# A tree-lookup layer on one Trainium2 core: five half-unit places for gathered rows, another order of the gathers, bias pieces kept elsewhere

## The reference, cut to what matters

```python
logits = x @ W_in.T + b_in                       # x: layer-normed tokens; HID = 4 trees x 1365 nodes x 4
act = gelu(logits); act4 = act.reshape(B, P, G, FAN)
decisions = argmax(act4, axis=-1)
for d in range(DEPTH):                            # DEPTH = 5 moves: 6 nodes for each token and tree
    moves = take_along_axis(decisions, current)
    current = next_platform + FAN * (current - platform) + moves
mask = sum(one_hot(n, G) for n in nodes)
new_logits = (act4 * mask[..., None]).reshape(B, HID) @ W_out.T
```

## Time and profile before

| | us |
|---|---|
| median of 3 runs | 2145.59 |
| lowest and highest | 2142.69, 2166.28 |
| the profiled execution | 2149.68 |
| its span in the profile | 2147.9 |
| from the first matmul of the trees layer to its last addition | 586.93 to 969.44 |

### The profile page before, as it was taken

The page is one execution under the profiler, slowest core; times in us unless marked ns, Lnnn a source line. Parts: engine busy times, 40 slices in busy tenths (PEclk is TensorE's granted clock), DMA queues, the critical chain, the costliest instruction groups (busy, mean ns, idle before and its releaser), DMA issues. The chain is left out here.

```text
span 2147.9 us, 34926 instructions
## 1 busy us (share of the span) xinstructions
PE 1648.2 (77%) x12368; PEld 1139.4 (53%) x12368; DVE 1221.2 (57%) x4315; ACT 850.6 (40%) x1792; POOL 464.6 (22%) x611
## 2 busy tenths in 40 slices
PE   3368646798878867745589979996886777999888
PEld 1147433454537656644345447763554654677666
DVE  5965645564277768642376623335766876766332
ACT  1142335355327556552245543332553420333423
POOL 0001000220022433420243100003201214655211
PEclk8655777799879988977699989986997866999979
DMA  2000001220034564640322000002211000000000
GB/s 80 0 11 1 9 29 46 71 57 19 7 112 164 207 227 158 225 169 6 102 75 76 22 16 0 0 27 64 54 33 58 1 1 1 2 2 2 2 1 21
DMA packets 79748, 115.69 MB, mean 54 GB/s; under 512 B 8416, under 2 KB 60512, under 8 KB 78816
## 3 DMA queue, kind: packets, MB, share of 16 engines
q0 software_dynamic: 18432, 67.38, 9.0%
q1 hardware_dynamic: 58560, 45.00, 7.5%
q10 hardware_dynamic: 2592, 1.18, 0.2%
HBM read 88.95 MB, written 1.05 MB: 42 GB/s over the span
## 5 line engine op out<-in xcount | busy, mean ns | idle before, releaser
L2321 POOL DMA_INDIRECT f_rows<-tree_table,f_index x128 | 132.7, 1037 | 324.8 <-DVE f_index L2377 153.4
L2534 PE MATMUL f_ps_o<-f_rows,shared_sb 128*128 128x128 f32 x1024 | 136.1, 299 | 71.0 <-ACT f_rows L2606 71.0
L2534 PEld LDWEIGHTS f_ps_o<-f_rows,shared_sb 128*128 128x128 f32 x1024 | 131.7, 212 | 76.7 <-ACT f_rows L2606 73.8
L1469 ACT ACTIVATE x_probs<-x_ps_z 128x768 f32<-128x768 f32 (+1 forms) x128 | 117.5, 918 | 104.6 <-PE x_ps_z L1334 66.4
L2606 ACT ACTIVATE f_rows<-f_rows,f_low_act 128x128 f32<-128x128 f32 x512 | 152.9, 387 | 0.8
L2416 DVE CUSTOM_DVE_ANT_0 f_rows<-f_rows,f_xn 128x128 f32<-128x128 f32 x512 | 111.4, 287 | 59.9 <-DMA f_rows<-tree_table,f_index 59.9
L1173 DVE TENSOR_REDUCE x_minus_max<-x_ps_s 128x4 f32<-128x1024 f32 x64 | 78.2, 1224 | 63.0 <-PE x_ps_s L1334 62.7
L3052 ACT ACTIVATE r_probs<-r_ps_z 128x768 f32<-128x768 f32 x64 | 51.9, 811 | 67.5 <-PE r_ps_z L2943 67.5
L1794 PE MATMUL f_ps_h<-f_xnT,weights 128*128 128x512 f32 x144 | 76.8, 661 | 2.3 <-ACT f_hT L1859 2.3
L1806 PEld LDWEIGHTS f_ps_y<-weights,f_hT 128*128 128x128 f32 x576 | 70.3, 193 | 14.3 <-issue 12.6
L1859 ACT ACTIVATE f_hT<-f_ps_h,weights 128x512 f32<-128x512 f32 x72 | 48.6, 685 | 69.8 <-PE f_ps_h L1794 68.1
(11 more groups left out here) (651 smaller groups left out, 4196.2 us busy)
## 6 DMA issues: line engine op xcount, KB each, us to landing
x_queries<-x_pieces SPq DMA_DIRECT2D x96, 64.0 KB, 2.1
x_keys<-x_pieces SPq DMA_DIRECT2D x84, 64.0 KB, 2.1
a_queries<-a_pieces SPq DMA_DIRECT2D x48, 64.0 KB, 2.1
weights<-w_L_ffn SPq DMA_DIRECT2D x1, 2985.5 KB, 10.1
a_keys<-a_pieces SPq DMA_DIRECT2D x42, 64.0 KB, 2.1
weights<-w_L_ffn SPq DMA_DIRECT2D x1, 2449.0 KB, 11.0
weights<-w_L_ffn SPq DMA_DIRECT2D x1, 2176.0 KB, 8.5
f_rows<-tree_table,f_index POOLq DMA_INDIRECT x128, 6.0
```

Source lines behind the costliest of these rows:

```text
L1469: a.activation(probs[:, r % HELD, :, :], ps_z[:, :, 0:WIDE], ACT.Exp, scale=scale).then_inc(exped, 1)
L2321: pool.indirect_dma_start(rows[:, u % 2, j, tree, :], None, g.tree_table, bass.IndirectOffsetOnAxis(index[:, u % 2, low, j * TREES + tree: ...
L2534: last = pe.matmul(ps_o[:, low, j, :], g.ident, rows[:, u % 2, j, tree, OUT + f * D:OUT + (f + 1) * D], start=k == 0, stop=k == TREES * FA ...
```

## The change

`rows` becomes a ring of five places, one half unit each, and the half (u, j) takes place (2u + j) mod 5, with a semaphore for each place. A gather for low = 0 into a place waits for the low = 1 sum of the half that held it five halves earlier. POOL's order becomes: gather(0,0,0), gather(0,0,1); then for each h gather(0,h+1,0), gather(1,h,0), gather(0,h+1,1), gather(1,h,1). `low_act` has three buffers instead of two. The bias pieces lose their own tiles: `bias_left` and `bias_part` lie in the fifth place of `rows`, `bias_rows` lies over the bias weights themselves, and so the bias is first copied to `bias_left`.

```diff
@@ -2258,6 +2258,7 @@
     LOW = DEPTH + 1 - DENSE
     OUT = FAN * D
     KEPT = 5
+    PLACES = 5
     STEPS = range(UNITS + 1)
     with ExitStack() as ctx:
         sb = lambda n, s, d=F32: ctx.enter_context(nc.sbuf_tensor("f1_" + n, s, d))
@@ -2266,14 +2267,16 @@
         xn, xnT = sb("xn", [P, KEPT, HALVES, D]), sb("xnT", [P, T])
         act = [sb("act%d" % d, [P, 2, Q, FAN ** d, FAN]) for d in range(DENSE)]
         here = [sb("here%d" % d, [P, Q, FAN ** d]) for d in range(1, DENSE)]
-        low_act = sb("low_act", [P, 2, Q, FAN])
+        low_act = sb("low_act", [P, 3, Q, FAN])
         value, rank_of = sb("value", [P, Q, FAN]), sb("rank_of", [P, Q, FAN])
         peak, node = sb("peak", [P, Q]), sb("node", [P, 2, Q])
         index = sb("index", [P, 2, LOW, Q], U32)
         maskedT = sb("maskedT", [P, ALL, P])
-        bias_rows, ones_rows = sb("bias_rows", [3, sum(WIDTHS)], BF16), sb("ones_rows", [3, P], BF16)
-        bias_left, bias_part, kept = sb("bias_left", [3, sum(WIDTHS)]), sb("bias_part", [3, sum(WIDTHS)]), sb("kept", [3, 3])
-        rows = sb("rows", [P, 2, HALVES, TREES, ROW])
+        ones_rows, kept = sb("ones_rows", [3, P], BF16), sb("kept", [3, 3])
+        rows = sb("rows", [P, PLACES, TREES, ROW])
+        bias_left, bias_part = (rows[0:3, PLACES - 1, :, :].rearrange("p t r -> p (t r)")[:, i * sum(WIDTHS):(i + 1) * sum(WIDTHS)]
+                                for i in range(2))
+        bias_rows = w["bias"][0:3, 0:sum(WIDTHS) // 2].bitcast(BF16)
         ps_t, ps_in, ps_d, ps_o = ps("ps_t", [P, 512]), ps("ps_in", [P, 3, 512]), ps("ps_d", [P, 4, D]), ps("ps_o", [P, LOW, 4, D])
         (xn_ready, xT_made, xnT_ready, in_made, act_ready, masked, mT_made, mT_ready, index_ready, dots_ready,
          low_ready, scaled, dense_summed, summed, dense_added, stats_taken, steps) = (
@@ -2305,30 +2308,34 @@
         trees_of = lambda j: slice(j * TREES, (j + 1) * TREES)
         tiles_in = lambda u: slice(u * HALVES, (u + 1) * HALVES)
         flat_act = lambda d, u, j: act[d][:, u % 2, trees_of(j), :, :].rearrange("p q c f -> p (q c f)")
-        gathered_in = lambda u, j: gathered[u % 2 * HALVES + j]
+        place = lambda u, j: (u * HALVES + j) % PLACES
+        gathered_in = lambda u, j: gathered[place(u, j)]
 
         @block.gpsimd
         def _(pool):
-            def gather(low, u):
-                for j in range(HALVES):
-                    pool.wait_ge(index_ready, pointed[low, u, j if low else 0] + 1)
+            def gather(low, u, j):
+                pool.wait_ge(index_ready, pointed[low, u, j if low else 0] + 1)
+                pool.sem_inc(may_gather, 1)
+                last_user = divmod(u * HALVES + j - PLACES, HALVES)
+                before = (0, u, j) if low else (1, *last_user)
+                if before in order_at:
+                    pool.wait_ge(summed, order_at[before] + 1)
                     pool.sem_inc(may_gather, 1)
-                    before = (0, u, j) if low else (1, u - 2, j)
-                    if before in order_at:
-                        pool.wait_ge(summed, order_at[before] + 1)
-                        pool.sem_inc(may_gather, 1)
-                    for tree in range(TREES):
-                        pool.indirect_dma_start(
-                            rows[:, u % 2, j, tree, :], None, g.tree_table,
-                            bass.IndirectOffsetOnAxis(index[:, u % 2, low, j * TREES + tree:j * TREES + tree + 1], 0),
-                        ).then_inc(gathered_in(u, j), 16)
-
-            gather(0, 0)
-            gather(0, 1)
+                for tree in range(TREES):
+                    pool.indirect_dma_start(
+                        rows[:, place(u, j), tree, :], None, g.tree_table,
+                        bass.IndirectOffsetOnAxis(index[:, u % 2, low, j * TREES + tree:j * TREES + tree + 1], 0),
+                    ).then_inc(gathered_in(u, j), 16)
+
+            gather(0, 0, 0)
+            gather(0, 0, 1)
             for h in range(UNITS):
-                gather(1, h)
-                if 2 <= h + 1 < UNITS:
-                    gather(0, h + 1)
+                if h + 1 < UNITS:
+                    gather(0, h + 1, 0)
+                gather(1, h, 0)
+                if h + 1 < UNITS:
+                    gather(0, h + 1, 1)
+                gather(1, h, 1)
 
         @block.vector
         def _(v):
@@ -2364,9 +2371,10 @@
                 v.memset(kept[:, 2:3], 0.0)
                 v.tensor_scalar(kept[:, 0:1], g.ident[0:3, 0:1], -1.0, 1.0, ALU.mult, ALU.add)
                 step(v.tensor_copy(kept[:, 1:2], g.ident[0:3, 2:3]))
-                step(v.tensor_copy(bias_rows[:, :], whole))
+                step(v.tensor_copy(bias_left[:, :], whole))
+                step(v.tensor_copy(bias_rows[:, :], bias_left[:, :]))
                 step(v.tensor_scalar(bias_part[:, :], bias_rows[:, :], kept[:, 2:3], kept[:, 0:1], ALU.subtract, ALU.mult))
-                step(v.tensor_tensor(bias_left[:, :], whole, bias_part[:, :], ALU.subtract))
+                step(v.tensor_tensor(bias_left[:, :], bias_left[:, :], bias_part[:, :], ALU.subtract))
                 step(v.tensor_copy(bias_rows[:, :], bias_left[:, :]))
                 step(v.tensor_scalar(bias_part[:, :], bias_rows[:, :], kept[:, 2:3], kept[:, 1:2], ALU.subtract, ALU.mult))
                 step(v.tensor_tensor(bias_left[:, :], bias_left[:, :], bias_part[:, :], ALU.subtract))
@@ -2408,20 +2416,20 @@
                 point(0, u, slice(0, Q))
 
             def dots(low, u, j):
-                v.wait_ge(gathered_in(u, j), (u // 2 * LOW + low + 1) * TREES * 16)
-                sums = low_act[:, u % 2, trees_of(j), :]
+                v.wait_ge(gathered_in(u, j), ((u * HALVES + j) // PLACES * LOW + low + 1) * TREES * 16)
+                sums = low_act[:, u % 3, trees_of(j), :]
                 for k in range(TREES * FAN):
                     tree, f = divmod(k, FAN)
-                    row = rows[:, u % 2, j, tree, f * D:(f + 1) * D]
+                    row = rows[:, place(u, j), tree, f * D:(f + 1) * D]
                     last = v.tensor_tensor_reduce(row, row, xn[:, u % KEPT, j, :], 1.0, 0.0,
-                                                  ALU.mult, ALU.add, low_act[:, u % 2, j * TREES + tree, f:f + 1])
+                                                  ALU.mult, ALU.add, low_act[:, u % 3, j * TREES + tree, f:f + 1])
                 step(last)
-                v.tensor_tensor(sums, sums, rows[:, u % 2, j, :, 2 * OUT:ROW], ALU.add).then_inc(dots_ready, 1)
+                v.tensor_tensor(sums, sums, rows[:, place(u, j), :, 2 * OUT:ROW], ALU.add).then_inc(dots_ready, 1)
 
             def go_down(u, j):
                 q = trees_of(j)
                 v.wait_ge(low_ready, order_at[0, u, j] + 1)
-                step(descend(low_act[:, u % 2, q, :], u, q))
+                step(descend(low_act[:, u % 3, q, :], u, q))
                 point(1, u, q)
 
             def add_dense(u):
@@ -2531,7 +2539,7 @@
                     pe.wait_ge(added[low], u)
                 for k in range(TREES * FAN):
                     tree, f = divmod(k, FAN)
-                    last = pe.matmul(ps_o[:, low, j, :], g.ident, rows[:, u % 2, j, tree, OUT + f * D:OUT + (f + 1) * D],
+                    last = pe.matmul(ps_o[:, low, j, :], g.ident, rows[:, place(u, j), tree, OUT + f * D:OUT + (f + 1) * D],
                                      start=k == 0, stop=k == TREES * FAN - 1)
                 last.then_inc(summed, 1)
 
@@ -2594,7 +2602,7 @@
                 last.then_inc(mT_ready, 1)
 
             def gelu_low(low, u, j):
-                part = low_act[:, u % 2, trees_of(j), :]
+                part = low_act[:, u % 3, trees_of(j), :]
                 a.wait_ge(dots_ready, order_at[low, u, j] + 1)
                 a.activation(part, part, ACT.Gelu).then_inc(low_ready, 1)
 
@@ -2602,8 +2610,8 @@
                 a.wait_ge(low_ready, order_at[low, u, j] + 1)
                 for k in range(TREES * FAN):
                     tree, f = divmod(k, FAN)
-                    row = rows[:, u % 2, j, tree, OUT + f * D:OUT + (f + 1) * D]
-                    last = a.activation(row, row, ACT.Copy, scale=low_act[:, u % 2, j * TREES + tree, f:f + 1])
+                    row = rows[:, place(u, j), tree, OUT + f * D:OUT + (f + 1) * D]
+                    last = a.activation(row, row, ACT.Copy, scale=low_act[:, u % 3, j * TREES + tree, f:f + 1])
                 last.then_inc(scaled, 1)
 
             for u in range(2):
@@ -3517,7 +3525,7 @@
         g.x = ctx.enter_context(nc.sbuf_tensor("x_tokens", [P, NT, D], F32))
         g.x_loaded = ctx.enter_context(nc.semaphore("x_loaded"))
 
-        g.gathered = [ctx.enter_context(nc.semaphore(f"gathered{j}")) for j in range(TILES)]
+        g.gathered = [ctx.enter_context(nc.semaphore(f"gathered{j}")) for j in range(TILES + 1)]
         first_stats = ctx.enter_context(nc.semaphore("first_stats"))
         stored = ctx.enter_context(nc.semaphore("stored"))
```

## The result

Thirteen runs of the changed kernel have a median of 2136.6 us against 2152.2 us for thirteen of the kernel before; the ratio is 0.9929, with a 95% interval of 0.9903 to 0.9955. So it is faster by 0.7%, about 15 us, where 41.9 us were forecast. The profiled executions say the same: 2134.28 against 2149.68, 15.4 us less.

What follows compares the result with a forecast made beforehand. DVE's 39.7 us of waits for gathered rows in steps 2 to 6 bound the layer; removing them, less new costs and waits, plus the tail brought dots(0,7,1) 41.9 us earlier: 2145.59 to 2103.7 us, range 2094 to 2121.

Steps and rivals of the forecast that it cites:

- No wait at dots(0,h,0): Start of each step: gather(0,h+1,0) leaves the loop, its rows are there a whole step early, no wait for h up to 7.
- The bias copy: One added f32 copy of 3 x 1360 on the path: 0.85 plus 0.05 of semaphore, 0.9 us (0.9 to 1.6).
- Landing: From the start of a gather's fourth issue to DVE's first use of the rows: 7.0 us, ends 6.5 and 7.6.
- rival 1: Landing grows with faster gather traffic: 5 us longer gives 2123 us, 8 us longer 2140; chance 0.09.
- rival 2: TensorE stays at the low clock: 2190 us if 0.5 throughout, chance 0.03; half as bad 2112 to 2120, chance 0.12.
- the tail: Step 6, no dense descent: dots(0,7,1) waits for gather(0,7,1), gated by the sum of (1,5,0), and starts at D + 35.5.
- The length of a step of DVE's work: One step without late rows: 34.8 us for steps 2 and 3, 34.1 for 4 and 5.
- The waits at dots(0,h,1): DVE's waits for rows of gather(0,h+1,1): 0, 0.4, 0.7 and 0.4 us in steps 3 to 6.
- The wait at dots(0,7,1): Step 6: DVE reaches dots(0,7,1) early and waits about 13 us for gather(0,7,1).
- The 1.7 us at dots(0,1,1): Start: gather(0,1,1) now stands behind gather(1,0,0), so its rows come 1.7 us late (0.9 to 2.4), on DVE's path.
- the gate of gather(0,h+1,1): Sum of (1,h-1,0) ends 26.3 us behind D, the start of dots(0,h,0); POOL then issues at D + 27.1.
- the sign of it: Listed sign of being wrong: a Gelu or `masked` wait setting steps of 38 us or more, PE then the limit.

Runs made afterwards that it cites:

- the first recording: The unchanged kernel before, in the profiled execution read for the forecast; 2149.68 us.
- the second: The unchanged kernel before, profiled again; ratio 1.0022 to the kernel before.

## Why the prediction was wrong

**Right.** *No wait at dots(0,h,0)* up to h = 7. *The bias copy* took 0.85 us, 0.89 with its gap. *Landing*: 753.30 to 759.72 is 6.4 us, so rival 1 did not come. *The clock*: 0.91 in steps 2 to 5, as hoped, so nor did rival 2. *The sums* take 3.84 alone and 7.41 in pairs. *The stretched issue*: one at 666.37 took 2.81. *The rest of the tail*: from dots(0,7,1) 42.9 us, before 43.2. *The length of a step of DVE's work*: 34.7 and 34.0 where nothing held it. Two agreements are luck. *The waits at dots(0,h,1)*, 0.9 to 1.1 us, were about as small as forecast only because both sides moved: the rows were usable 5.6 us later in the step than forecast, and DVE wanted them 4.9 later. *The wait at dots(0,7,1)*, 14.0 where about 13 was expected, is one between rows and dots that both came about 8 us late. *The 1.7 us at dots(0,1,1)* did not show: the late update of the dots before it, 4.90 us, hid it.

**The step that failed** is the gate of gather(0,h+1,1), "8.8 + 3.7 + 3.2 + 3.1 + 7.5 = 26.3, and 0.8 to POOL: D + 27.1", and with it "Without late rows DVE's own work is the next limit". Both take each engine to go on as soon as the one before it has ended. That held in the trace that I read. Of the terms of the gate only the first failed: in step 3 Gelu and scaling, 8.8 us in the sum, became 16.7 us to the start of sum(0,3,0). ACT's 8.00 us of waiting put Gelu at D + 10.0 instead of D + 3.7, and PE's turn and dense sum ended 1.7 us behind the scaling. The other four, 769.45 to 786.68, took 17.2 us where 17.5 were forecast. In the changed order a run of issues lies across D, where PE hands over to ACT and DVE to itself, and there the handing over costs up to 5.6 us. In numbers, with 25.8 us too little at dots(0,7,1):
- the steps 2 to 5: 150.6 us instead of 140.1. DVE's update, 1.95 us in step 3 and 1.65 to 2.4 in the others, the rows 1.07 late and the smaller gaps beside them make 12.8 in the four steps (in before's step 1 there are none); less the 2.5 that were forecast of waits this is 10.3 of the 10.5.
- step 1: 40.6 instead of 35.5, so 5.1. POOL issued sixteen in a row, 661.4 to 683.0, and the dots of (0,1,0) crept through their later part; their own update then came 4.90 us late, 2.1 behind the run's end.
- the start, to D of step 1: 1.5 more than forecast, 0.84 of it there before the layer's bias work began.
- the tail: dots(0,7,1) at D + 44.2 instead of D + 35.5, so 8.7. `take_masked` stood 14.04 us under a run of twelve (861.0 to 875.9), and gather(0,7,1) began at 898.80, D + 33.2, where D + 24.8 was forecast. Here the update came 0.7 us before the run's end, at 875.21:

```profile
875.23 1.24 ACT L2598 ACTIVATE f_maskedT<-f_ps_in 128x1280 f32<-128x1280 f32 x1 [14.04 <-remote]
```

The text named the sign of it ("a wait at Gelu or at `masked` that sets steps of 38 us or more") and gave it no chance. Of the run of twelve in the trace of before it asked only when its rows land, not what it does to the other engines; the first recording shows nothing there, and the second shows that such a run can hold updates.

**Shown**: that the rest of the change gains nothing without the new order; that updates of PE which fall into the later part of an unbroken run of issues mostly wait for its end plus 1.0 to 2.0 us, that DVE's come late there too, and ACT's do not; that this does not hang on the bytes; that breaking such a run, with nothing else changed, gained about 21 us with six places; and that the gate of gather(0,h+1,1) fell late by the waits that these updates make. **Argued only**: that this accounts for the whole of the missing 26 us. The sums fit, but no version with five places was free of it. **Open**: by what path POOL's issues hold the updates of PE and DVE, and why the first recording of before shows none late. That recording is also the only one with all 2048 landing records of the gathers; the other 19 have 1031 to 1469 of them, and all 19 have late updates. So I can't exclude that writing the records itself has a part in the lateness, or is held by the same thing. All times here, medians too, are of executions that left records; an unrecorded one was not measured.

## What to carry to other kernels

When gathers are moved off a critical wait, look at where their issues now stand and not only at when their rows land: runs of eight and more issues (10 us and more) across the points where the engines hand over to each other went with 25.8 us less gain at dots(0,7,1) than the 41.9 forecast. A wait that breaks the run at a moment when nobody needs POOL can be worth more than another buffer: six places alone gave 0.988, six places with one more wait 0.978. With five places the same kind of wait gained nothing clear (0.9913), since the issues joined into a new run elsewhere. And read a second recording of the kernel before, for waits with the releaser "remote": a cost that falls into another wait's shadow doesn't show until that wait is gone.

## What the hardware showed

- Semaphore updates of PE in the later part of an unbroken run of indirect-gather issues mostly come behind its end: by about 1.1 us for four issues, 1.2 to 1.5 for six, 1.6 to 2.0 for eight, and 1.8 to 2.8 for twelve, where some also come before the end. DVE's own are 1 to 5 us late there, some of them while the run still goes on. PE's in the first 5 us of a run were on time in the changed kernel.
- ACT's own updates are on time there, in every trace.
- An issue that DVE's 2.29 us product stretches (2.92 instead of 0.94 us) seems to act as a break in the run: a sum that ended 5.9 us behind the first issue was then on time, and 5.6 us late in runs without such an issue.
- In the same stretch DVE's dots, else one per 0.21 us, have idle gaps of 0.4 to 1.1 us.
- Halving the bytes of each row leaves PE's updates as late.
- The first recording of the kernel before, one of twenty, shows no late update and no such gaps.
